# Gather passes of layers 1 and 3 over fixed spans of 128 sorted blocks, summed in a PSUM bank that a register addresses

## The chip, the cores and the metric

The program is one kernel on one core of one Trainium2 chip. It does a whole graph network in one launch. The metric is the device time of an execution in microseconds (us). The kernel before took 3753.84 us, the median of three runs (3752.54 to 3764.85).

The engines are TensorE (PE in the profile, PEld for its weight loads), VectorE (DVE), ScalarE (ACT), GpSimd (POOL) and SyncE (SP). Each runs its own instruction stream and waits for the others through semaphores. A "q" behind a name, as in PEldq, means the engine's sequencer: register loads, address arithmetic, branches.

## The reference, cut to what matters

There are 6250 nodes of 128 features and 100000 edges with source, target, 128 attributes, a type out of three and a weight. Four layers are computed one after the other:

```
v   = segment_sum(edge_attr, src) / count                 # layer 0, then an MLP with batch norm
agg = segment_sum(x[src], dst) / degree                   # layer 1
msg = [x[src], x[dst]] @ Wmsg[edge_type]                  # layer 2
agg = segment_sum(msg, dst) / count
out = segment_sum(dinv[src] * w * dinv[dst] * (x @ W)[src], dst)   # layer 3
```

After each layer come a residual sum and a layer norm. All values are fp32. What matters here is `x[src]` (a gather by source node) and `segment_sum(..., dst)` (a reduction by target node), done once per layer for all edges.

## The kernel before, in words

Nodes lie in 49 groups of 128. An edge belongs to a pair (source group, target group); the edges of a pair are packed into blocks of four. Two DRAM tables hold the blocks: `slots`, sorted by source group, and `gbuf`, sorted by target group. There are at most 26801 blocks. First a placement pass (to 1103 us in the trace) scatters all edges into `slots`, with POOL's indirect DMAs.

A tile is 128 consecutive blocks of a table. Tiles are cut so that each belongs to one group: a group's first tile begins at the group's first block, and its last tile runs over into the next group's blocks. With 49 groups that makes 258 tiles (`TILES`), handled in 43 rounds (`RR`) of 6 (`RING`). Blocks of a tile that aren't the group's own get the address NOWHERE in `to_blk`, and the indirect DMA drops them.

The stages that the change touches are these:

- `reduce(0)`, from about 1110 us: tiles of `slots` are loaded by SP. POOL's `keep_lanes` writes each edge's lane (its source node within the group) into `dst_lane`. DVE and ACT turn lanes into one-hot matrices, PE multiplies and DVE adds to `sums`. Beside that ACT's `keep_pays` copies each tile's payload (8 numbers an edge) into `pays`; one tile in six has its one-hot made by ACT (`scalar_hots`).
- `gather(1)`, from 1467.8 us, and `gather(3)`, from 3086.9 us: for each tile DVE makes a one-hot out of lanes that SP loads again from `lane_rows`. PE waits for the one-hot (`src_hots`) and for a free PSUM bank (`staged`), and does four 128x128 fp32 matmuls into bank r, each one a complete result (`start=True, stop=True`). ACT copies the bank into a ring of six row buffers (for layer 1 with the payload beside it, for layer 3 scaled by the edge's weight). POOL issues one indirect DMA that scatters the 128 rows to their blocks in `gbuf` (`scatter_block`, L804; it prints as `to_blk`). ACT takes a row buffer again when its send has landed (`sent`).
- `gather(2)` is the same by edge type, with bf16 parts. The change leaves it as it is.
- `reduce(1)`, `reduce(2)`, `reduce(3)` read tiles of `gbuf`.

PE has to know which node group a tile belongs to. The number differs with the input, so it comes out of a table in SBUF. At the head of each round of six tiles, `loaded(at_x, ...)` brings six values into PE registers. In the trace that is a TENSOR_LOAD on PE's sequencer (L501). The loop over 43 rounds is a hardware loop (`pe.Fori`), one round an iteration, so the order in the program is: register load, then six times (address arithmetic, waits, four matmuls), then the branch. DVE and SP do register loads of the same kind in the `reduce` stages (`at_sum`, `at_blk`).

## Time and profile before

| | |
|---|---|
| median of 3 timed runs | 3753.84 us |
| span of the profiled execution, first to last instruction | 3754.1 us (the profile gives no other time of it) |
| PE / DVE / POOL / ACT busy | 75% / 67% / 50% / 40% |
| mean granted TensorE clock | 0.961 |
| gather(1): first matmul to start of last send | 1467.8 to 1806.4 us |
| gather(3): first matmul to start of last send | 3086.9 to 3434.0 us |

The profile is one execution. A group of instructions is a row with the line, engine, operation, operands, count, busy time and mean duration, and behind the bar the idle time of the engine before them and what ended it. PE's fp32 matmuls appear as two records each, so one tile of `gather(1)` is 8 records. A row of one source line's instructions gives the minimum, median and maximum duration in ns, and the first and last start.

### The profile page before, as it was taken

What the parts mean: (1) busy time and instruction counts of PE and PEld (TensorE: products, weight loads), DVE (VectorE), ACT (ScalarE), POOL (GpSimd) and SP (SyncE); (2) the same over time, 40 slices, a digit from 0 to 9 for tenths busy, and PEclk for the clock granted to TensorE, in tenths of its full rate; (3) what the DMA queues carried; (4) which work ended last, traced back from release to release, by engine and by line L of the source; (5) the groups of instructions that cost most, each with busy time, mean ns of one, the idle gap of its engine ahead of it and who ended that gap; (6) DMA issues with size and microseconds to landing.
All of it is one profiled execution on the core that took longest, in us unless ns stands there. A gap on an engine that the chain in (4) does not pass through costs nothing.

```text
span 3754.1 us, 95326 instructions
## 1 busy us (share of the span) xinstructions
PE 2826.7 (75%) x23184; PEld 2448.4 (65%) x23185; DVE 2500.2 (67%) x7099; ACT 1518.9 (40%) x4337; POOL 1873.3 (50%) x2268
## 2 busy tenths in 40 slices
PE   8555544444439986778799799999999957777996
PEld 6232322222229965777799479999888957777995
DVE  7666666666647778555577777777666776554667
ACT  0111000000004445555576543222365347887665
POOL 4777777777763342777434344444432007774000
PEclk9999999999999998999899899999999969998998
DMA  6444444444449933888697035555477817786883
GB/s 214 151 149 144 146 149 141 149 143 147 148 130 290 291 128 118 279 275 277 221 290 255 9 127 180 173 183 177 136 226 235 263 38 269 275 275 197 286 281 122
DMA packets 419029, 721.55 MB, mean 192 GB/s; under 512 B 68624, under 2 KB 198169, under 8 KB 417932
## 3 DMA queue, kind: packets, MB, share of 16 engines
q1 hardware_dynamic: 330492, 494.35, 43.0%
q0 software_dynamic: 88464, 226.43, 16.0%
q14 instruction: 52, 0.43, 0.0%
q8 instruction: 21, 0.34, 0.0%
HBM read 481.26 MB, written 285.09 MB: 204 GB/s over the span
## 4 chain that ended last, share of the span: by engine, by line
PE 39%; POOL 23%; issue 14%; DMA 12%; DVE 5%; ACT 3%; SPq 2%; DVEq 1%; POOLq 1%; ACTq 0%
POOL slots L750 19%; PE ps L1379 18%; PE ps L1412 9%; DMA gbuf<-ring_raw,to_blk 8%; PE ps L1414 5%; POOL gbuf L804 4%; DMA ring_raw<-gbuf 3%; PE ps L1254 2%; PE ps L1465 1%; PE ps L1456 1%; SPq L501 1%; SPq L622 1%; DVE stats L1930 1%; PE ps L1521 1%; DVEq L501 1%
## 5 line engine op out<-in xcount | busy, mean ns | idle before, releaser
L804 POOL DMA_INDIRECT gbuf<-ring_raw,to_blk x774 | 754.2, 974 | 728.9 <-DVE ring_raw L1863 261.9
L750 POOL DMA_INDIRECT slots<-ring_raw,idx_edges x782 | 751.4, 961 | 242.3 <-issue 242.3
L1379 PE MATMUL ps<-ring_raw,memory 128*128 128x128 f32 (+2 forms) x6576 | 783.9, 279 | 84.9 <-DVE memory L1831 49.4
L1379 PEld LDWEIGHTS ps<-ring_raw,memory 128*128 128x128 f32 x6576 | 763.3, 192 | 113.1 <-issue 60.3
L1831 DVE TENSOR_TENSOR memory<-dst_lane,lane_ids 128x512 f32<-128x512 f32 x774 | 539.6, 698 | 73.3 <-POOL dst_lane L768 51.1
L1290 PE MATMUL ps<-memory 128*49 128x343 bf16 (+6 forms) x784 | 263.5, 489 | 387.9 <-DVE memory L1727 386.6
L1412 PE MATMUL ps<-memory 128*128 x2752 | 497.7, 273 | 10.2 <-DVE memory L1872 8.0
L1841 DVE TENSOR_TENSOR memory<-memory,ps 128x128 f32 (+2 forms) x1032 | 293.4, 284 | 314.7 <-PE ps L1379 302.6
L936 ACT ACTIVATE memory<-lane_ids,dst_lane 128x128 f32<-128x128 f32 x1032 | 331.0, 395 | 400.3 <-PE ps L1379 263.1
L1414 PE MATMUL ps<-memory 128*128 x2752 | 477.5, 220 | 0.0
L1290 PEld LDWEIGHTS ps<-memory 128*49 128x49 bf16 x784 | 113.9, 159 | 530.7 <-DVE memory L1727 301.9
L1424 PE MATMUL ps<-memory 128*128 x2064 | 270.2, 292 | 88.2 <-ACT ring_raw L977 49.9
L888 ACT COPY ring_raw<-memory 128x49 f32 (+1 forms) x112 | 26.0, 232 | 767.5 <-DMA slots<-ring_raw,idx_edges 767.4
L1424 PE MATMUL ps<-X,memory 128*128 x2064 | 267.0, 290 | 78.3 <-DVE memory L1886 31.0
L1424 PEld LDWEIGHTS ps<-memory 128*128 128x128 f32 x2064 | 255.8, 203 | 102.7 <-issue 101.3
L1424 PEld LDWEIGHTS ps<-X,memory 128*128 128x128 f32 x2064 | 252.8, 202 | 92.7 <-issue 91.8
L977 ACT ACTIVATE ring_raw<-ps,edge_w 128x128 f32<-128x128 f32 x1032 | 277.7, 407 | 68.9 <-issue 48.8
L1412 PEld LDWEIGHTS ps<-memory 128*128 128x128 bf16 x2752 | 269.8, 98 | 47.1 <-issue 15.2
L980 ACT COPY ring_raw<-ps 128x512 f32<-128x512 f32 x258 | 151.3, 586 | 361.9 <-PE ps L1414 361.9
L1863 DVE TENSOR_TENSOR ring_raw<-ring_raw,ps 128x512 f32<-128x512 f32 x258 | 177.5, 688 | 144.7 <-ACT ring_raw L980 144.7
L1414 PEld LDWEIGHTS ps<-memory 128*128 128x128 bf16 x2752 | 269.1, 98 | 2.4
L1886 DVE TENSOR_TENSOR memory<-memory,ps 128x512 f32<-128x512 bf16 x252 | 173.5, 689 | 112.4 <-PE ps L1424 112.4
(283 smaller groups left out, 4801.6 us busy)
## 6 DMA issues: line engine op xcount, KB each, us to landing
ring_raw<-gbuf SPq DMA_DIRECT2D x669, 268.0 KB, 3.7
ring_raw<-in_edge_attr SPq DMA_DIRECT2D x111, 448.0 KB
ring_raw<-slots SPq DMA_DIRECT2D x153, 272.0 KB, 4.0
zr<-lane_rows SPq DMA_DIRECT2D x87, 384.0 KB
zt<-lane_rows SPq DMA_DIRECT2D x87, 384.0 KB
memory<-lane_rows SPq DMA_DIRECT2D x84, 384.0 KB
memory<-slots SPq DMA_DIRECT2D x105, 272.0 KB, 4.0
memory<-gbuf SPq DMA_DIRECT2D x105, 268.0 KB, 3.8
```

The lines of the kernel that those rows point to most:

```text
L750: pool.indirect_dma_start(edges, bass.IndirectOffsetOnAxis(idx_edges[0:n, u, j:j + 1], 0), edge_rows[0:n, u, j, :], None).then_inc(scatter ...
L804: pool.indirect_dma_start(gbuf, bass.IndirectOffsetOnAxis(to_blk[:, t:t + 1], 0), node_rows[:, r, :], None, bounds_check=NBLK - 1, oob_is_ ...
L936: ins = act.activation(hots[:, r, j * P:(j + 1) * P], lane_ids[:, :], ACT.Abs, bias=dst_lane[:, bass.ds(at, 1)], scale=-1.0)
L977: ins = act.activation(rows[:, j, 0:D], parts[:, j, :], ACT.Copy, scale=edge_w[:, bass.ds(at * BLK + j, 1)])
L1290: ins = pe.matmul(counts_of(s)[:, j * GROUPS:].rearrange("p (n g) -> p n g", g=GROUPS), hot2[:, u, 0, :, j], hot2[:, u, 1, :, j][:, None, ...
L1379: ins = pe.matmul(bank(r % 3, width), hots[:, r, j * P:(j + 1) * P], rows[:, j, 0:width], start=j == 0, stop=j == BLK - 1)
L1412: pe.matmul(to.rearrange("p (k d) -> p k d", d=D), hot, msgs[:, 0:2, bass.ds(at[r] + t * D, D)], start=t == 0, stop=False, skip_group_chec ...
L1414: ins = pe.matmul(to[:, D:2 * D], hot, msgs[:, 2, bass.ds(at[r] + t * D, D)], start=False, stop=t == TYPES - 1, skip_group_check=True)
L1424: ins = pe.matmul(bank(r)[:, j * P:(j + 1) * P], hots[:, r, j * P:(j + 1) * P], nodes[:, bass.ds(at[r], D)], start=True, stop=True)
L1831: dve.tensor_tensor(hots[:, r, :].rearrange("p (k d) -> p k d", d=P), lane.broadcast_to([P, BLK, P]), lane_ids[:, None, :].broadcast_to([P ...
L1841: dve.tensor_tensor(to, to, bank(r % 3, width), ALU.add).then_inc(added, 1)
L1863: dve.tensor_tensor(rows, rows, pair_bank(r)[:, :, 0:D], ALU.add).then_inc(staged, 1)
```

## The change

Source tiles are no longer cut at group bounds. A span is 128 blocks of `slots` counted from 0, so there are 210 spans (`SPANS`). A span that holds blocks of two or more groups is worked on in several steps, one for each group; the steps of all spans are 258 again. Every step's matmuls add to the span's PSUM bank (`start=False`). The bank is emptied before, by a one-column matmul with `start=True` (`new_bank`), which each step issues for the bank after its own. Only when the last step of a span is done does ACT copy it and POOL send it: 35 rounds (`SR`) of 6 sends.

The mapping from step to span differs with the input, so four things that were constants or single loads now come from tables through registers: the bank that a step adds to (`at_bank`), the bank to empty (`at_next`), the number of sends that must be done (`free`), and on ACT the number of steps after which a span is whole (`span_steps`). The wait for a free bank now asks for the span five before, not six. Rows of `slots` and the payload grow from 8 to 9 numbers an edge (the ninth is the source lane with the type in it, so that a POOL pass over types goes). `keep_pays` writes by span and saves the target address of each tile first.

```diff
-PAY = 8
-P_ONE, P_TYPE, P_W, P_DST, P_SRC, P_TO = 0, 1, 4, 5, 6, 7
+PAY = 9
+P_ONE, P_TYPE, P_W, P_DST, P_SRC, P_TYPED, P_TO = 0, 1, 4, 5, 6, 7, 8
...
             def keep_pays(h, odd):
                 i = h * 2 + odd
+                at = loaded(at_pay, None, i, ACT_E, (SPANS - 1) * BLK * PAY)
                 for r in range(RING):
                     rows = rows_of(0, r, odd).rearrange("p (k w) -> p k w", k=BLK)
                     wait_rows(act, 0, h, r, odd)
-                    act.copy(pays[:, bass.ds(i * RING + r, 1), :].rearrange("p a (k w) -> p (a k) w", k=BLK),
+                    act.copy(to_of[:, bass.ds(i * RING + r, 1)], rows[:, 0, D + P_TO:D + P_TO + 1])
+                    act.wait_ge(pays_kept, i * RING + (RING + r))
+                    act.copy(pays_raw[:, bass.ds(at[r], BLK * PAY)].rearrange("p (k w) -> p k w", k=BLK),
                              rows[:, :, D:ROW_A]).then_inc(pays_kept, 1)
...
-                def send_tiles(i):
+                def send_round(i):
+                    steps = loaded(span_steps[layer], None, i, ACT_E, RING + GATHERED[3] + TILES)
                     for r in range(RING):
                         at = i * RING + r
-                        act.wait_ge(gathered, i * RING + (RING + base + r + 1))
+                        act.wait_ge(gathered, steps[r])
...
-                for i in range(RR):
+                for i in range(RR if layer == 2 else SR):
                     for r in range(RING):
                         scatter_block(i, r)
...
-                def gather_tiles(i):
+                def new_bank(to):
+                    pe.matmul(ps_flat[:, to], ident_h[:, :], none_h, start=True, stop=True, skip_group_check=True)
+
+                def gather_steps(i):
                     at = loaded(at_x, None, i, PE, (GROUPS - 1) * D)
+                    to = loaded(at_bank, None, i, PE, (RING - 1) * 512)
+                    upon = loaded(at_next, None, i, PE, (RING - 1) * 512)
+                    free = loaded(spans_free[layer], None, i, PE, STAGED[3] + SPANS + 2)
                     for r in range(RING):
+                        pe.wait_ge(staged, free[r])
+                        new_bank(bass.ds(upon[r], 1))
                         pe.wait_ge(src_hots, i * RING + (base + r + 1))
-                        pe.wait_ge(staged, i * RING + (base + r + 1))
                         for j in range(BLK):
-                            ins = pe.matmul(bank(r)[:, j * P:(j + 1) * P], hots[:, r, j * P:(j + 1) * P],
-                                            nodes[:, bass.ds(at[r], D)], start=True, stop=True)
+                            ins = pe.matmul(ps_flat[:, bass.ds(to[r] + j * D, D)], hots[:, r, j * P:(j + 1) * P],
+                                            nodes[:, bass.ds(at[r], D)], start=False, stop=j == BLK - 1,
+                                            skip_group_check=True)
                         ins.then_inc(gathered, 1)
```

The rest of the diff makes the tables on DVE after the placement pass (`span_tables`, some 20 operations on at most 258 columns), splits `send` into `send_spans` and `send_typed`, and moves waits to the new counts (`STAGED`).

On PE, at the head of a round of `gather(1)` and in its first tile, this stands in the program before. ISA is address arithmetic on the sequencer, often with a wait:

```order
L501 TENSOR_LOAD at_x
L1421 REGISTER_ALU
L1424 ISA [waits staged,src_hots]
L1424 MATMUL ps<-X,memory 128x128 x4
L1421 REGISTER_ALU
L1424 ISA [waits staged,src_hots]
L1424 MATMUL ps<-X,memory 128x128 x4
```

And this stands there in the changed program. The four loads are `at_x`, `at_bank`, `at_next` and `free`, which all lie in one tensor's partitions and so print as `at_x`:

```order
L532 TENSOR_LOAD at_x
L532 ISA
L532 TENSOR_LOAD at_x
L532 ISA
L532 TENSOR_LOAD at_x
L532 ISA
L532 TENSOR_LOAD at_x
L1470 ISA [waits staged]
L1470 MATMUL ps<-none,ident_h 128x1
L1480 REGISTER_ALU
L1482 ISA [waits src_hots]
L1482 MATMUL ps<-X,memory 128x128
```

One load at the head of a round became four in a row, and each step got a small matmul and an ISA before each of its four matmuls. The second place is ACT's `keep_pays` in `reduce(0)`. Two tiles of it before:

```order
L948 ISA [waits rows_in0]
L948 COPY memory<-ring_raw 128x32
L948 ISA [waits rows_in1]
L948 COPY memory<-ring_raw 128x32
L948 ISA [waits rows_in2]
```

And the head of a round and two tiles of it now:

```order
L532 TENSOR_LOAD at_msg
L441 ISA
L986 ISA [waits rows_in0]
L986 COPY memory<-ring_raw 128x1
L987 REGISTER_ALU
L988 ISA [waits pays_kept]
L988 COPY memory<-ring_raw 128x36
L986 ISA [waits rows_in1]
L986 COPY memory<-ring_raw 128x1
L987 REGISTER_ALU
L988 ISA [waits pays_kept]
L988 COPY memory<-ring_raw 128x36
```

A register load stands ahead of the round, each tile has two copies, and the second waits until the payload copy before it is done.

## Rows read from the trace of the kernel before

**Rows 1.** The page's head.
```profile
span 3754.1 us, 95326 instructions
```

**Rows 2.** Both gathers, reduce(0), gather(2): busy us by engine, clock, DMA share, GB/s.
```profile
1466.00:1798.00 332.00, 266.98 (x2064) 252.78 (x2064) 177.56 (x259) 173.24 (x511) 243.84 (x251) 0.94 0.78 265
3085.00:3444.00 359.00, 273.62 (x2080) 259.15 (x2081) 197.78 (x323) 281.45 (x1042) 251.77 (x258) 0.92 0.73 249
1108.00:1358.00 250.00, 239.70 (x2028) 233.43 (x2029) 187.77 (x467) 114.62 (x465) 85.11 (x258) 1.00 0.90 287
2177.00:2700.00 523.00, 518.40 (x6164) 475.86 (x6165) 380.86 (x1029) 168.32 (x305) 248.69 (x256) 0.99 0.50 170
```

**Rows 3.** Timeline of both gathers: first matmuls, POOL's sends, the last ones.
```profile
1467.82 6.40 PE L1424 MATMUL ps<-X,memory 128*128 x34 [17.79 <-DVE memory L1886]
...
1475.99 0.97 POOL L804 DMA_INDIRECT gbuf<-ring_raw,to_blk  x1 [0.31 <-issue]
1477.27 0.97 POOL L804 DMA_INDIRECT gbuf<-ring_raw,to_blk  x1 [0.30 <-issue]
...
1806.41 0.97 POOL L804 DMA_INDIRECT gbuf<-ring_raw,to_blk  x1 [0.31 <-issue]
...
3086.90 6.29 PE L1424 MATMUL ps<-memory 128*128 x38 [21.46 <-DVE memory L1886]
...
3433.96 0.97 POOL L804 DMA_INDIRECT gbuf<-ring_raw,to_blk  x1 [0.30 <-issue]
```

**Rows 4.** Timeline of PE in gather(1), 1640 to 1662 us.
```profile
1641.31 1.15 PE L1424 MATMUL ps<-X,memory 128*128 x8 [0.63 <-ACT ring_raw L985]
1643.91 4.73 PE L1424 MATMUL ps<-X,memory 128*128 x40 [1.45 <-DVE memory L1886]
```

**Rows 5.** PE's sequencer by line, 1641.3 to 1643.9 us: min/median/max ns, first and last start.
```profile
L501 PEldq TENSOR_LOAD <-at_x x1: 1753/1753/1753, 1641.8 to 1641.8; - x1
L1421 PEldq ALU_OP  x1: 36/36/36, 1643.6 to 1643.6; - x1
```

**Rows 6.** Register loads of gather(1), gather(3), gather(2), and of DVE in reduce(0) (two single ones first).
```profile
L501 PEldq TENSOR_LOAD <-at_x x43: 819/1526/2653, 1466.4 to 1787.7; - x43
L501 PEldq TENSOR_LOAD <-at_x x43: 822/1730/2961, 3085.7 to 3416.9; - x43
L1430 PEldq TENSOR_LOAD <-at_msg x21: 846/895/1249, 2177.7 to 2665.1; - x21
L501 DVEq TENSOR_LOAD <-at_sum x1: 820/820/820, 1138.8 to 1138.8; - x1
L501 DVEq TENSOR_LOAD <-at_sum x1: 1407/1407/1407, 1144.5 to 1144.5; - x1
L501 DVEq TENSOR_LOAD <-at_sum x43: 811/1069/1427, 1114.3 to 1357.6; - x43
```

**Rows 7.** Waits of gather(2), 2256 to 2632 us: total us, times, longest.
```profile
PEld ps L1412 <- issue: 5.3, 15, 0.7
```

**Rows 8.** Weight loads of gather(2), 2256 to 2632 us.
```profile
L1412 PEld LDWEIGHTS ps<-memory 128*128 128x128 bf16 x1985 | 194.2, 98 | 27.9 <-issue 5.3
```

**Rows 9.** Timeline of ACT in reduce(0), 1200 to 1212 us.
```profile
1201.44 1.28 ACT L936 ACTIVATE memory<-lane_ids,dst_lane 128x128 f32<-128x128 f32 x4 [2.72 <-PE ps L1379]
1202.75 0.72 ACT L940 ACTIVATE memory<-memory,ones 128x512 f32<-128x512 f32 x1
1203.38 0.68 ACT L948 COPY memory<-memory 128x32 f32 x5
1207.49 1.28 ACT L936 ACTIVATE memory<-lane_ids,dst_lane 128x128 f32<-128x128 f32 x4 [3.31 <-PE ps L1379]
```

**Rows 10.** Timeline: POOL's first scatter, then DVE's last table, POOL's last scatter.
```profile
85.14 1.21 POOL L734 DMA_INDIRECT slots<-memory,zero_idx  x1 [50.43 <-issue]
...
1085.16 0.32 DVE L1814 TENSOR_SCALAR at_sum<-back 1x258 int32<-1x258 f32 x1
...
1102.84 0.88 POOL L750 DMA_INDIRECT slots<-ring_raw,idx_edges  x1 [0.30 <-issue]
```

More of the change, by code:

```diff
@@ L58 @@
 HALVES = 2 * RR
+SPANS = -(-MAXB // P)
+SR = SPANS // RING
+assert SR * RING == SPANS and SPANS + GROUPS - 1 == TILES and SPANS * P <= NBLK
+assert all((t * 171) >> 10 == t // RING for t in range(SPANS))
 SCALAR_HOTS = ((5,), (2, 5), (5,), (2, 5))
@@ L497, in tile_cols @@
         def tile_cols(table, k, i, n=RING, span=RING):
-            return table[0:1, k, bass.ds(i * span, n)] if k is not None else table[0:1, bass.ds(i * span, n)]
+            return table[:, k, bass.ds(i * span, n)] if k is not None else table[:, bass.ds(i * span, n)]
         def loaded(table, k, i, engine, top, span=RING):
@@ L1072, in _ @@
                 normalise_step(X, i, x1_ready, Y_CUT)
-            send(1)
+            send_spans(1)
             target_hots(1)
@@ L1151, in _ @@
                 parts(i, i + 1 if i + 1 < STEPS else None)
-            send(2)
+            send_typed()
             def own_in(i, first, count=2):
@@ L1230, in _ @@
                 ins.then_inc(st["g3"]["z"], 1)
-            send(3)
+            send_spans(3)
             act.wait_ge(gathered, RING + GATHERED[3] + TILES)
```

225 lines of the change are left out of this document (145 added, 80 removed).

## The prediction, made before the changed kernel was timed

> **What bounds the kernel now.** I read four views in this order. First the page and the time by stage. The page's span is 3754.1 us [rows 1], 0.3 us from the median of the runs shown, so the sum is made against the span and carried over to the median as it is. In the stretches [rows 2] the two gathers that change are those where neither PE nor the DMA engines are full: PE is busy 267 of 332 us and 274 of 359 us, the DMA share is 0.78 and 0.73. `gather(2)` for comparison has PE busy 518 of 523 us.
>
> Second the timeline of POOL [rows 3]. A send starts every 1.28 us (1475.99, 1477.27): 0.97 us of work and 0.30 us between. 258 of those make 330 us, and from the first matmul to the start of the last send it is 338.6 us in `gather(1)` (1467.8 to 1806.4) and 347.1 us in `gather(3)` (3086.9 to 3434.0). So POOL's issue of sends sets the pace, and fewer sends can only help as far as nobody else is near that pace.
>
> Third, who is near: PE. Its matmuls for one tile take 0.895 us: 40 records in 4.73 us and 8 records in 1.15 us [rows 4], so 32 records in 3.58 us. Six tiles are 5.37 us, and a round of six sends is 7.67 us. That looks like 2.3 us of room in each round. The timeline shows that most of it isn't room: between the 8 records and the 40 there is a hole of 1.45 us, in every round.
>
> Fourth, what the hole is. PE's sequencer [rows 5] starts the register load at 1641.8 and holds it for 1.753 us. The next instruction, the arithmetic of line 1421 that only computes a count to wait for, starts at 1643.6, right behind the load. So the load blocks everything behind it in the stream. The matmuls of the tile before end at 1642.46, and the first of the next starts at 1643.91, 0.4 us after the load. The profile puts the hole down to VectorE, whose one-hots are six tiles ahead; it is the load. PE's round is therefore 5.37 + 1.45 = 6.8 us out of 7.67. PE has 0.85 us of room in a round, and not 2.3.
>
> **The change, part by part. Sends.** 210 times 1.28 us are 268 us a gather, 62 us less than 330. This is what the change could give at most in each. Bytes don't fall: the blocks that were dropped from a tile moved no data, and every block is written once either way. The DMA engines' busy time is 0.78 x 332 = 259 us; at the share of 0.90 that `reduce(0)` reaches [rows 2] it fits in 288 us.
>
> **Register loads on PE.** Each round's one load becomes four in a row, with an address instruction between. What does one cost? In the two gathers the median is 1.53 and 1.73 us, with 0.82 as the least and 2.96 as the most [rows 6]. DVE's loads of six values in `reduce(0)` are two kinds, 0.82 and 1.41 us (the two single rows; all 43 have the median 1.07), which alternate from round to round. The mean of the two kinds is 1.11 us. So six 4-byte values cost 1.11 us on the average in a quieter stage, and some 1.63 us (mean of the two medians) in these gathers, where the load shares the way into SBUF with sends and lane loads. After the change the same bytes are spread over more time, so I take a value nearer to the quiet end, 1.25 us; the ends 1.11 and 1.63 are kept for the range.
>
> The Trainium skill, DMA: Bandwidth & Descriptors, section Latency and other measured facts, gives about 600 ns as the floor of a `tensor_load`; no load here reaches it, the least being 0.81 us. The skill's Runtime: NRT & Kernel Launch, section Instruction fetch mechanics, puts such loads at about 200 ns a register even in bulk, which would make 2.4 us of `gather(2)`'s loads of twelve; the trace disagrees with 0.895 us for them. By that rule four loads would be 4.8 us a round, and the sum below would end at about 4000 us.
>
> **How much of them is covered.** PE's array goes on with queued matmuls while the sequencer loads. In `gather(2)`, where PE is full as it will be here, a load of 0.895 us and 0.4 us of restart leave a hole of 5.3 / 15 = 0.35 us [rows 7]. So 0.94 us is covered. In the row of `gather(1)` it was 0.7 us. I take 0.94.
>
> **Matmuls of a step.** There are still 258 steps of four matmuls. Each gets `new_bank` besides, one bf16 weight load and one column. The nearest rows: 98 ns for a bf16 weight load [rows 8], and 518.4 us / 6164 = 84 ns a matmul in full flow [rows 2]. Value 84 ns, bounds 0 (beside other work) and 182 ns. Six make 0.5 us a round. The granted clock is 0.94 and 0.92 in these gathers, that is some 12% to 16% of the time at 1.2 GHz; six steps then take (5.37 + 0.5) x 1.065 = 6.25 us. The address instructions between the matmuls are about 0.12 us each on the sequencer, by estimate: three instructions stand in the 0.36 us between the load's end and the first matmul [rows 4, 5]. Four are 0.5 us in the 0.98 us of a step's matmuls: covered, as the sequencer is ahead.
>
> **The sum.** A round is 6.25 + 4 x 1.25 + 0.3 (three address instructions) + 0.4 (restart) - 0.94 = 11.0 us, against 7.67 now. 43 rounds are 473 us, and 1.5 us to the start of the last send: 475 us. Against 338.6 and 347.1 us that is 136 and 128 us more, 264 together. POOL needs 4.9 x 1.28 = 6.2 us of the 11 in a round and idles. ACT needs 1.1 us a send in `gather(3)`, where it is busiest, 5.3 us of the 11, and its own new load of about 1.25 us a round of sends fits as well. DVE's one-hots wait for PE. The shallower bank ring (five spans, not six) costs nothing while PE is last: during the 5 us hole the sends drain.
>
> **`reduce(0)`.** ACT works from 1201.44 to 1204.2 and then idles 3.31 us of a round of 6.05 us [rows 9]. The second copy per tile is another 0.21 us, and the wait for the copy before it costs perhaps 0.15 us: 6 x 0.36 = 2.2 us, and the load of 0.8 to 1.4 us, partly beside the 0.72 us activation ahead of it. About 2.9 us against 3.31: hidden, cost 0. If the cover fails, with the load at 1.41 us and twice the waits, it is 0.9 us x 43 = 39 us. Rows of `slots` grow by 4 bytes in 544, 0.7%: nothing while POOL's issue sets the placement's pace and PE that of `reduce(0)`, at most 0.7% of the 1350 us of both, 9 us. The tables: DVE has its last at 1085.5, POOL's last scatter is at 1102.8 [rows 10], and some 20 operations of 0.4 us, 8 us, fit between. POOL's two more payload operations lie ahead of a stretch of 50.4 us in which it idles [rows 10]. Together I put 3 us.
>
> 3754 + 264 + 3 = 4021; I forecast 4020 us. With loads of 1.11 us a round is 10.4 us, and the end is 3970; without `new_bank` and at full clock 0.88 us a round less, 76 us, about 3895. With loads of 1.63 us a round is 12.5 us and the end is 4150. The likeliest case's own range is 3890 to 4150.
>
> **Rivals.** First, on the other side: the four loads overlap, because each only reads SBUF and the address instruction between doesn't need its value. Then they cost one load and three times 0.1 us; with 1.6 us for that load the round is 6.25 + 1.6 + 0.3 + 0.4 - 0.94 = 7.6 us, a gather is 327 + 1.5 us, and the end is 10 + 18 us under now: 3725 us. With a load of 1.1 us it is 3685, and the DMA engines would stop it at about 3650. It decides from the point where the four together cost less than some 2 us. For it speaks that no row has two loads back to back. Against it speak the rows of the sequencer [rows 5]: an instruction that doesn't use the value and yet waited until the load's end.
>
> Second, loads at the page's floor of 0.6 us: the mechanism stays, but as a short stall. From the rows this is the case where loads back to back are cheaper than single ones: 4 x 0.6 = 2.4 us, a round of 8.4 us, 24 and 16 us more a gather, 3795 us. The Trainium skill's DMA page (its section named above) has that floor; no row reaches it.
>
> Third, the gain and the loss meet: loads overlap in part, some 2 us for the four, and the time stays within 0.3% (11 us) of 3754.
>
> Fourth, on top of the forecast: ACT becomes the bound in `reduce(0)`, 39 us more, about 4060 us. It wants waits twice as dear as taken, and moves the time inside the forecast's range.
>
> **How the numbers follow.** Serial loads (with or without the fourth) 0.81, the cheap serial ones 0.04, overlapping ones 0.11, a draw 0.04. Faster by over 0.3% is the overlap, 0.11; within 0.3%, which is about what a measurement of this kernel can tell from no change, 0.04; slower 0.85. The range from 3790 to 4140 leaves out the overlap and the draw, 0.15, and some 0.05 at the ends.
>
> **What would show it.** In the changed profile PE's sequencer should have four register loads in a row at each of 43 rounds, each starting when the one before has ended, and the array should stand still some 4 to 5 us behind them. POOL's sends should come in bursts with idle between, its idle time before sends more than 150 us a gather above now, and PE's matmuls from the first to the last should take some 470 us. The stretches of `gather(2)`, the three later reductions and the placement should be as now. It is wrong if the four loads start together or if a round takes under 8 us; then the first rival holds. If the round is about 11 us but `reduce(0)` has grown by over 10 us, the fourth holds as well.

## The result, and the profile after

The changed kernel takes 4345.9 us (median of 4 runs, 4343.3 to 4356.2), the kernel before beside it 3753.2 us (4 runs): 1.158 times as long, 95% interval 1.157 to 1.160. I had forecast 4020 us, with a range that ended at 4140. The direction was right and the size was wrong by more than half: 593 us more, where 266 were forecast.

The page of the changed kernel: span, granted clock in 40 slices, and PE's two kinds of matmul in the gathers (busy us, mean ns | idle before, and what ended it).

```profile
span 4345.0 us, 98074 instructions
...
PEclk9999999999999777777899999999998677777998
...
L1470 PE MATMUL ps<-none,ident_h 128*128 128x1 bf16 x518 | 96.0, 185 | 544.8 <-issue 507.0
...
L1482 PE MATMUL ps<-X,memory 128*128 x2064 | 364.8, 350 | 3.4
```

Two stretches of sevens in the clock row are new; they are the two gathers. 507 us of PE's idle time stand before the matmul that opens a round, put down to "issue": nothing was waited for but the instruction itself. Both gathers, `reduce(0)` and `gather(2)`, to be held against [rows 2]:

```profile
1481.00:2102.00 621.00, 372.06 (x2319) 353.90 (x2320) 173.94 (x252) 144.37 (x417) 201.23 (x207) 0.73 0.41 141
3392.00:4024.00 632.00, 377.94 (x2318) 359.27 (x2318) 193.53 (x308) 230.24 (x833) 200.49 (x207) 0.73 0.40 138
1114.00:1372.00 258.00, 246.86 (x2059) 239.39 (x2060) 191.83 (x470) 169.67 (x731) 83.34 (x257) 1.00 0.87 278
2478.00:3001.00 523.00, 520.63 (x6186) 477.36 (x6186) 379.46 (x1023) 168.91 (x306) 249.33 (x256) 1.00 0.51 170
```

`gather(2)` is as it was (523 us). The gathers of layers 1 and 3 are 621 and 632 us instead of 332 and 359, and their clock fell from 0.94 and 0.92 to 0.73. From the first matmul to the start of the last send it is 624.0 and 636.6 us (before 338.6 and 347.1 [rows 3]): 285 and 290 us more, 575 of the 593. `reduce(0)` grew by 6.6 us from its first matmul to its last, and the placement by 3.6 us.

The timeline of PE in one round (start, us, x records, [idle before]), against [rows 4]:

```profile
1741.90 0.18 PE L1470 MATMUL ps<-none,ident_h 128*128 128x1 bf16 x1 [4.79 <-issue]
1742.20 2.08 PE L1482 MATMUL ps<-X,memory 128*128 x8
...
1744.14 2.06 PE L1482 MATMUL ps<-X,memory 128*128 x8
...
1746.06 1.83 PE L1482 MATMUL ps<-X,memory 128*128 x8
...
1747.76 1.14 PE L1482 MATMUL ps<-X,memory 128*128 x8
1748.73 0.17 PE L1470 MATMUL ps<-none,ident_h 128*128 128x1 bf16 x1
1748.76 1.14 PE L1482 MATMUL ps<-X,memory 128*128 x8
...
1749.77 1.14 PE L1482 MATMUL ps<-X,memory 128*128 x8
1757.77 0.18 PE L1470 MATMUL ps<-none,ident_h 128*128 128x1 bf16 x1 [6.86 <-issue]
```

The first three steps behind the hole start 1.9 us apart, the last three 1.00 us apart. The windows of those pieces give the reason, in the column of the granted clock (third from the end):

```profile
1741.90:1747.70 5.80, 5.68 (x27) 5.47 (x28) 1.38 (x2) 1.40 (x4) 0.97 (x1) 0.51 0.14 55
1747.70:1750.60 2.90, 2.90 (x28) 2.87 (x28) 2.04 (x3) 0.72 (x3) 1.94 (x2) 1.00 0.56 191
1750.60:1757.70 7.10, 0.30 (x3) 0.11 (x1) 0.72 (x2) 1.27 (x4) 1.94 (x2) 0.76 0.62 218
1757.70:1761.50 3.80, 3.68 (x18) 3.54 (x19) 0.69 (x1) 0.70 (x2) 0.00 (x0) 0.54 0.00 0
```

The clock is at its full level (2.4 GHz) at the end of a round, drops to the half (1.2 GHz) within the hole, and stays there while the next steps already run. The loads of that hole and of the whole of both gathers (min/median/max ns), against [rows 5, 6]:

```profile
L532 PEldq TENSOR_LOAD <-at_x x4: 1646/1947/2297, 1749.3 to 1756.0; - x4
...
L532 PEldq TENSOR_LOAD <-at_x x168: 826/1656/2762, 1487.3 to 2091.4; - x168
...
L532 PEldq TENSOR_LOAD <-at_x x126: 818/1806/2960, 3398.3 to 4012.6; - x126
...
L532 PEldq TENSOR_LOAD <-at_msg x42: 1456/1744/2812, 3406.0 to 4014.0; - x42
```

They run one after the other. Over the 43 rounds of `gather(1)` four loads span 7.28 us on average (1.70 us each), the array rests 5.82 us, and the six steps take 8.75 us: a round of 14.57 us. POOL's sends come in bursts as forecast:

```profile
1738.87 0.97 POOL L840 DMA_INDIRECT gbuf<-ring_raw,group_raw  x1 [0.30 <-issue]
1745.99 0.97 POOL L840 DMA_INDIRECT gbuf<-ring_raw,group_raw  x1 [6.15 <-ACT ring_raw L1021]
```

So my mechanism stood, and two sizes in it didn't: 4.76 us of rest were forecast and 5.82 measured, 6.25 us of steps forecast and 8.75 measured. The theory that I then tested: the loads dominate, directly and through the clock. Its rivals: `new_bank` between the steps, or something else of the change (tables, spans, ACT's waits).

### The profile page after: what moved, and what is told of

It reads as the page before. It is cut to its first block, busy times and chain, and to the rows that moved or that the text cites. A ratio compares the mean times of both kernels' runs of the same rounds, so it can differ in the third digit from the quotient of the medians.

```text
span 4345.0 us, 98074 instructions
## 1 busy us (share of the span) xinstructions
PE 3041.8 (70%) x23700; PEld 2652.2 (61%) x23701; DVE 2510.6 (58%) x7118; ACT 1497.6 (34%) x4308; POOL 1769.2 (41%) x2172
## 4 chain that ended last, share of the span: by engine, by line
PE 49%; issue 19%; POOL 17%; ACT 4%; DMA 3%; DVE 3%; SPq 2%; ACTq 1%; DVEq 1%; POOLq 0%
POOL slots L784 17%; PE ps L1430 16%; PE ps L1482 14%; PE ps L1463 8%; PE ps L1465 4%; DMA ring_raw<-gbuf 3%; ACT ring_raw L1017 2%; PE ps L1304 1%; PE ps L1525 1%; PE ps L1516 1%; SPq L532 1%; DVE stats L2021 1%; SPq L653 1%; PE ps L1581 1%; PE ps L1554 0%
## 5 line engine op out<-in xcount | busy, mean ns | idle before, releaser
L840 POOL DMA_INDIRECT gbuf<-ring_raw,group_raw x420 | 409.0, 974 | 1128.4 <-ACT ring_raw L1017 587.5
L1922 DVE TENSOR_TENSOR memory<-lane_pair,lane_ids 128x512 f32<-128x512 f32 x774 | 541.5, 700 | 77.9 <-POOL lane_pair L807 22.8
L1463 PE MATMUL ps<-memory 128*128 x2752 | 498.1, 273 | 10.1 <-DVE memory L1963 7.7
L1465 PE MATMUL ps<-memory 128*128 x2752 | 477.5, 220 | 0.0
L1470 PE MATMUL ps<-none,ident_h 128*128 128x1 bf16 x518 | 96.0, 185 | 544.8 <-issue 507.0
L973 ACT ACTIVATE memory<-lane_ids,lane_pair 128x128 f32<-128x128 f32 x1032 | 330.9, 395 | 312.7 <-PE ps L1430 244.9
L1017 ACT ACTIVATE ring_raw<-ps,lane_pair 128x128 f32<-128x128 f32 x840 | 232.2, 381 | 411.3 <-PE ps L1482 397.4
L1482 PE MATMUL ps<-memory 128*128 x2064 | 371.1, 354 | 2.6
L1482 PE MATMUL ps<-X,memory 128*128 x2064 | 364.8, 350 | 3.4
L840 POOL DMA_INDIRECT gbuf<-ring_raw,to_blk x258 | 251.6, 975 | 277.5 <-DVE ring_raw L1954 263.3
L1482 PEld LDWEIGHTS ps<-memory 128*128 128x128 f32 x2064 | 350.6, 256 | 13.6 <-issue 0.2
L1463 PEld LDWEIGHTS ps<-memory 128*128 128x128 bf16 x2752 | 269.7, 98 | 47.2 <-issue 15.3
```

Of the source, the lines that this page charges most:

```text
L840: pool.indirect_dma_start(gbuf, bass.IndirectOffsetOnAxis(to[:, t:t + 1], 0), node_rows[:, r, :], None, bounds_check=NBLK - 1, oob_is_err= ...
L973: ins = act.activation(hots[:, r, j * P:(j + 1) * P], lane_ids[:, :], ACT.Abs, bias=dst_lane[:, bass.ds(at, 1)], scale=-1.0)
L1017: ins = act.activation(rows[:, j, 0:D], parts[:, j, :], ACT.Copy, scale=edge_w[:, bass.ds(at * BLK + j, 1)])
L1463: pe.matmul(to.rearrange("p (k d) -> p k d", d=D), hot, msgs[:, 0:2, bass.ds(at[r] + t * D, D)], start=t == 0, stop=False, skip_group_chec ...
L1465: ins = pe.matmul(to[:, D:2 * D], hot, msgs[:, 2, bass.ds(at[r] + t * D, D)], start=False, stop=t == TYPES - 1, skip_group_check=True)
L1482: ins = pe.matmul(ps_flat[:, bass.ds(to[r] + j * D, D)], hots[:, r, j * P:(j + 1) * P], nodes[:, bass.ds(at[r], D)], start=False, stop=j = ...
```

## The experiments

**One part each, in the kernel before.** `head3` puts four loads of `at_x` at the head of a gather round, `head1` two, `spread3` also four but ahead of tiles 0, 1, 3 and 4; `newbank` adds the bank-opening matmul alone.

```diff
-                    at = loaded(at_x, None, i, PE, (GROUPS - 1) * D)
+                    sets = [loaded(at_x, None, i, PE, (GROUPS - 1) * D) for _ in range(4)]
+                    at = [sets[r % 4][r] for r in range(RING)]
```

> The kernel before, with four register loads of the node table in a row at the head of each round of the two gathers in place of one; nothing else (258 sends, no bank matmul). Theory A (serial loads, and a clock that falls in the long hole): a round is as long as in the changed kernel, some 14 us, both gathers grow by about 280 us each, 4300 us in all, and the granted clock in them is near 0.73. Theory B (serial loads, clock no part of it): matmuls at their present pace, round 5.7 + 4 x 1.7 + 0.4 - 0.9 = 12 us, 516 us a gather, about 4100 us. Theory C (the loads overlap or are hidden, and the bank matmul or the address instructions between matmuls are what costs): within 50 us of 3753.

> The kernel before with two register loads in a row at the head of each round of the two gathers. Two loads of 1.6 us leave a hole of about 2.7 us. If the clock stays at some 0.93: round 5.7 + 3.2 + 0.4 - 0.9 = 8.4 us, 361 us a gather, about 3790 us. If a hole of that length already brings the clock down as in the changed kernel: round 5.37 x 1.4 + 2.7 = 10.2 us, 439 us a gather, about 3940 us. Theory C: no change.

> The kernel before with four register loads a round, but one each ahead of tiles 0, 1, 3 and 4 and not all at the head. As many loads as in the run with three more at the head, in four short holes. Each load of 1.7 us and 0.4 us of restart has up to 0.9 us covered by queued matmuls: four holes of 1.2 us, round 5.7 + 4.8 = 10.5 us, 452 us a gather, about 3965 us, with the clock near 0.9. Theory A says it is at least 200 us faster than with all four at the head, since the clock stays up; theory B says that it differs only by the cover, 3 x 0.9 x 86 = 230 us at the most, at an equal clock. If the clock here is near 0.73 as well, then it is the share of idle time and not the length of one hole that counts.

> The kernel before with the one-column matmul ahead of each tile's four and those four adding to the bank (start=False); one register load a round, 258 sends. Theories A and B: six times 84 ns fit in PE's 0.85 us of room in a round, within 15 us of 3753. Theory C: much of the 590 us, at least 200 us.

The rest is the mean over the rounds of `gather(1)`. The first three kernels were timed twice each, `newbank` eight times.

| | median us | ratio (95%) | rest of the array a round | clock in gather(1) |
|---|---|---|---|---|
| head3 | 4169.8 | 1.111 (1.107 to 1.114) | 5.24 us | 0.76 |
| head1 | 3811.8 | 1.015 (1.010 to 1.021) | 2.15 us | 0.89 |
| spread3 | 3848.0 | 1.025 (1.022 to 1.028) | 2.3 us, in pieces | 0.93 |
| newbank | 3754.0 | 1.000 (0.999 to 1.001) | as before | 0.96 |

The same four loads cost 413 us at the head and 91 us spread out. The window 1481 to 1781 us of `head3`, then of `spread3`:

```profile
1481.00:1781.00 300.00, 175.44 (x1104) 171.25 (x1104) 94.71 (x138) 95.67 (x276) 133.88 (x138) 0.76 0.49 164
```

```profile
1481.00:1781.00 300.00, 225.01 (x1609) 205.26 (x1609) 138.07 (x201) 139.46 (x400) 194.22 (x200) 0.93 0.70 239
```

Four loads in a row thus cost 70% as much as the whole change without anything else of it, and the clock falls with the long rest. The 322 us between `head3` and `spread3` aren't the clock alone. Between its own instructions PE's sequencer stands still in `head3` for 4.0 us a round (pauses over 0.15 us counted), while the array works off its steps; in `spread3` it hardly ever does. There it works from end to end, beside the array, and its loads and arithmetic make the round. I had expected four holes of 1.2 us and 3965 us; it was 3848. `newbank` costs nothing while the sends set the pace. Does it still cost nothing behind the loads? `head3bank` has both:

```diff
+                        pe.matmul(bank(r)[:, 0:1], ident_h[:, :], none_h, start=True, stop=True,
+                                  skip_group_check=True)
...
-                                            nodes[:, bass.ds(at[r], D)], start=True, stop=True)
+                                            nodes[:, bass.ds(at[r], D)], start=False, stop=j == BLK - 1,
+                                            skip_group_check=True)
```

> The kernel before with both costs that the change put on TensorE, and nothing else of the change: four register loads in a row at the head of every gather round, and a one-column matmul that opens each tile's bank ahead of its 49 or fewer slice matmuls, which then all add up. Sends, tables and banks stay as before. Theory A (what the change costs is the four loads with the low clock after them, and in the rounds that are now bound by TensorE the bank-opening matmul and the longer steps): about 86 rounds x 0.6 us more than with the four loads alone (4169.75 us), so about 4220 us (4190 to 4260), with about 125 us of the changed kernel's time left for its address instructions, its waits on the register-held send counts and its other stages. Rival B (the bank matmul is free here as it was alone): 4170 us. Rival C (the bank matmul's break between the steps is what brings the clock further down, from 0.77 to 0.73): about 4330 us.

(A tile's matmuls in this kernel are four, and not "49 or fewer".) 4237.7 us, ratio 1.130 (1.128 to 1.132), clock 0.75: 68 us over `head3`, 0.79 us a round. An instruction that is free in one kernel is paid for once its engine is last: six times 84 ns would be 0.5 us at full clock. A round takes 13.44 us here (loads 6.26, all else 7.18) against 14.57 in the changed kernel (7.28 and 7.29). 1.13 us times 86 rounds is 97 of the 108 us still missing, and nearly all of it is load time again: the fourth table has 16-bit values (1.79 us a load by its position, against 1.35), and the others take 1.66 us on average against 1.57.

**The clock by itself.** `warm6` is the changed kernel with six matmuls of 512 columns, read by nobody, ahead of the loads.

```diff
+                    for _ in range(6):
+                        pe.matmul(bank(6), ident[:, :], wcat[:, 0:4, :].rearrange("p g d -> p (g d)"), start=True, stop=True,
+                                  skip_group_check=True)
```

> The changed kernel with six matmuls of 512 columns, whose result nothing reads (they go into the sixth bank), issued ahead of the four register loads of each gather round, so that the array has work while the sequencer loads. Theory A (the low clock in the gathers comes from the array's long rest in each round): with the rest filled by some 5 us of work, the granted clock in the gathers goes from 0.73 to above 0.9, the array part of a round from 8.75 to about 6.3 us, the round from 14.6 to about 12.2 us, and the program takes about 4140 us (4090 to 4200), though it does more work. Rival B (the clock doesn't answer to the rest but to something else, as the loads themselves): the clock stays at 0.73, the junk lies beside the loads, and the time stays at 4350 us or rises by up to the junk's own 5 us a round (4780 us). Rival C (loads wait until the array has emptied): the junk adds its 5 us to each round and the clock rises; the time is about 4350 - 200 + 430 = 4580 us.

```profile
1481.00:1781.00 300.00, 265.84 (x1443) 192.61 (x1442) 90.66 (x133) 72.61 (x210) 100.78 (x104) 0.94 0.44 152
```

4297.0 us, ratio 1.145 (1.143 to 1.148): more work, and 49 us less. The array's rest is 1.48 us, the clock 0.94, and what remains of a round of 13.82 us behind rest and 5.3 us of added work is 7.0 us for the six steps in place of 8.75. That the clock answers to the rest is shown. My number was too hopeful (4140), because the added matmuls took the place of the steps that had been queued beside the loads: the last step ends 0.7 us after the first load has begun, in the changed kernel 1.65 us after, so each round lost about 1 us of cover.

**`reduce(0)`.** `pays` is the kernel before with ACT's extra copy and wait.

```diff
+                    act.copy(local0[:, bass.ds(i * RING + r, 1)], rows[:, 0, D + P_TO:D + P_TO + 1])
+                    act.wait_ge(pays_kept, i * RING + (RING + r))
```

> The kernel before with only the extra copy and the extra wait on ScalarE in the loop that keeps the pay columns, as in the changed kernel, and nothing else. Theory A (the first reduction is bound by ScalarE's loop, so that the copy and the wait make it longer): the first reduction's matmuls take about 258 us in place of 251.7, and the program about 3760 us. Rival B (those 6.6 us come from the ring's changed send order or the tables): the stage stays at 251.7 us and the program at 3754 us.

3755.5 us, ratio 1.001 (1.000 to 1.002), and the stage's matmuls take 251.3 us, as before: theory A fell. The 6.6 us of the changed kernel come from something else in that stage (longer rows, ACT's register load or the ring's order); which, wasn't tried.

**What a load costs.** Fewer loads should be cheaper, I thought. `table1` packs the four tables into one of 16-bit values with one load of 24 values a round, `table2` has two loads of twelve, and `word1` packs three tables as 4-byte values into a load of 18, with the 16-bit load of six behind it.

```diff
-                    at = loaded(at_x, None, i, PE, (GROUPS - 1) * D)
-                    to = loaded(at_bank, None, i, PE, (RING - 1) * 512)
-                    upon = loaded(at_next, None, i, PE, (RING - 1) * 512)
-                    free = loaded(spans_free[layer], None, i, PE, STAGED[3] + SPANS + 2)
+                    got = []
+                    for q in range(LOADS):
+                        got += nc.values_load_multi_w_load_instructions(
+                            at_pe_all[0:1, bass.ds(i * (PER * RING) + q * PER * TILES, PER * RING)], engines=[PE],
```

> The changed kernel with its four PE tables packed in one 16-bit table, so that one register load a round brings all 24 values (layer 3 adds its offset to the send count on the sequencer); everything else of the change stays. Theory A: a load costs by the load and not by the value, so the hole is that of the kernel before, about 1.5 us, the clock is back above 0.9, a round is 6.2 + 1.6 + 0.4 - 0.9 = 7.3 us against 7.67 before, a gather is 316 us; with the 10 us that placement and the first reduction have grown the end is 3753 - 22 - 31 + 10 = 3710 us. If a register costs 0.2 us: a load of 4.8 us, round 10.5 us and more, 3950 us or above. Theory C (bank matmul, address instructions): no less than 4200 us.

> The same with two loads of 12 values each a round. Two loads of 1.6 us: hole 2.9 us, round 6.2 + 3.2 + 0.5 - 0.9 = 9.0 us if the clock stays above 0.9, 388 us a gather, 3753 + 49 + 41 + 10 = 3853 us; with the clock at 0.75 another 1.5 us a round, 3980 us.

> The changed kernel, but its three tables of addresses for TensorE (node column, bank, next bank) are laid side by side as 4-byte values, eighteen a round in one register load; the table of send counts stays 16-bit and is loaded by a second load of six values. Two register loads a round in place of four, and as many values. Theory A (a load of 4-byte values costs little more with eighteen values than with six: twelve take 0.9 us elsewhere in this program): the two loads take about 1.0 to 2.5 and 1.7 us, the array's hole is about 3 us in place of 5.8, the granted clock in the gathers rises from 0.73 to about 0.88, a round takes about 9.5 us in place of 14.6, and the program takes about 3930 us (3850 to 4020). Rival B (the price goes with the values, whatever their width, as it did with the 16-bit tables): the loads take 7 us together as before, and the time stays at about 4350 us. Rival C (sharing a table's place with other engines' tables costs more): slower than 4360 us.

They took 4348.5, 4367.6 and 4242.4 us (ratios 1.157, 1.163 and 1.131, each within 0.003). The one load of `table1`:

```profile
L1484 PEldq TENSOR_LOAD <-at_pe x86: 5671/7502/8320, 1475.1 to 4007.9; - x86
```

and two loads of eighteen 4-byte values of `word1`, in neighbouring rounds:

```profile
L1477 PEldq TENSOR_LOAD <-at_all x1: 5205/5205/5205, 1916.5 to 1916.5; - x1
...
L1477 PEldq TENSOR_LOAD <-at_all x1: 1768/1768/1768, 1930.9 to 1930.9; - x1
```

The expectation of a price per load was wrong: 24 16-bit values take 7.5 us in one load and 7.6 us in the two of `table2` (3.9 and 3.5 us; on average, in `gather(1)`), 0.31 us a value. The changed kernel's four loads, three of 4-byte values and one of 16-bit values, take 7.28 us. The 4-byte values are cheap in every second round and dear in the others. A round's 72 bytes begin at a multiple of 16 only every second time; the six values of 24 bytes behind DVE's turns of 0.82 and 1.41 us [rows 6] do the same. `pad8` tests this: the changed kernel with eight places for six values, so that every round begins at a multiple of 32 bytes.

```diff
-            mark(dve.tensor_scalar(at_x, groups_on[0:1], float(D), -float(D), ALU.mult, ALU.add))
+            mark(dve.tensor_scalar(padded(at_x), by_round(groups_on[0:1]), float(D), -float(D), ALU.mult, ALU.add))
```

> The changed kernel with the same four loads of six values a round, but each table has eight places for a round in place of six, so that a round's values begin at a multiple of 32 bytes (16 in the 16-bit table) and not, in every second round, 8 bytes beside one. Theory A (a load whose values begin off a multiple of 16 bytes costs nearly double: 1.4 against 0.8 us on VectorE and 2.2 against 1.1 us on TensorE, by turns): all rounds are like today's even ones, the four loads take 5.0 us in place of 7.3, the rest of the array 3.6 us in place of 5.8, the clock is about 0.8, the round about 11.8 us, and the program about 4110 us (4050 to 4180). Rival B (the turns come from something else that goes by two rounds, as the buffers or the sends): the loads go on by turns and the time stays at 4345 us.

4256.9 us, ratio 1.133 (1.131 to 1.134). The turns are gone (means of the three 4-byte loads 1.41, 1.08 and 1.23 us, alike in even and odd rounds), the four loads span 6.26 us in place of 7.28, and 89 us are back. It is less than forecast, as the 16-bit load stays at 2.0 us:

```profile
L1481 PEldq TENSOR_LOAD <-at_x x301: 813/1306/2643, 1476.5 to 3922.3; - x151
...
L1481 PEldq TENSOR_LOAD <-at_msg x43: 1467/1993/2785, 3350.8 to 3923.7; - x43
```

**Where the loads stand.** With 16-bit values: `half2` moves the second of `table2`'s two loads ahead of the fourth step; `step6` has six loads of four, each ahead of its step.

```diff
                     for r in range(RING):
+                        if r % AHEAD == 0:
+                            got = nc.values_load_multi_w_load_instructions(
+                                at_pe_all[0:1, bass.ds(i * (4 * RING) + 4 * r, 4 * AHEAD)], engines=[PE],
```

> As the kernel with all loads at the head of the round in two loads of twelve 16-bit values (4367.59 us), but the second of them stands ahead of the fourth step instead of behind the first. Theory A (what is loaded beside issued work costs about 1.5 us less a round, and a rest of some 2 us instead of 5.8 leaves more of the clock): each load takes 3.6 us as before, the array rests twice for 2.2 us, the clock is about 0.85, the round about 12.2 us, the program about 4150 us (4080 to 4230). Rival B (where the loads stand makes no difference, TensorE's sequencer being the bound from end to end): 4370 us. Rival C (each rest brings its own slow steps behind it, now twice a round): the clock stays at 0.73 or falls, and the time is 4300 us or more.

> The changed kernel with TensorE's four tables laid step by step in one table of 16-bit values, and a register load of the four values of one step (node column, bank, next bank, sends) ahead of each step, six loads of four values a round in place of four loads of six values at its head. As many values are loaded; only where they are loaded differs. Theory A (the price goes with the values, some 0.3 us each, and the array's queue of issued matmuls covers about 1 to 1.5 us of a load): each load takes about 1.3 us, a step of the sequencer about 2.0 us, the array rests for some 1 us between steps instead of 5.8 us at once, so that the granted clock stays above 0.9; a round takes about 12.0 us in place of 14.6, the program about 4130 us (4050 to 4200). Rival B (a load has a floor of about 1.7 us here, however few its values): 2.4 us a step, a round 14.5 us, and the time stays at about 4340 us in spite of the clock. Rival C (many short rests bring the clock down as a long one does): clock 0.75 and about 4250 us or more.

`half2`: 4144.5 us, ratio 1.105 (1.103 to 1.106), clock 0.82: 223 us less than `table2` for the place alone, as theory A had it. `step6`: 4225.9 us, ratio 1.126 (1.124 to 1.128), clock 0.83 in `gather(1)` and 0.75 in `gather(3)`. I had expected short rests to keep the clock above 0.9; they don't, and rival C is nearer in its number. But the clock no longer sets the time in these two. PE's sequencer stands still for 3.0 us (`gather(1)`) and 2.2 us (`gather(3)`) a round in `table2`, counted as above, and for at most 0.2 us in `half2` and `step6`: what was gained is time in which it had stood still beside the array's slow steps. A round of `step6` is 13.0 us, six loads of 1.18 us and six times 0.99 us of all else on the sequencer, where I had taken 0.7. Why the clock falls so far with some 3.0 us of rest a round in four pieces, below what `spread3` has with 2.3 us in three, stays open. Both gathers of `step6`:

```profile
1481.00:1950.00 469.00, 345.18 (x1953) 290.08 (x1953) 149.66 (x218) 121.46 (x350) 169.68 (x175) 0.83 0.48 163
3292.00:3750.00 458.00, 331.05 (x1749) 281.28 (x1747) 177.86 (x343) 185.95 (x632) 146.01 (x151) 0.75 0.43 148
```

**Cheap loads.** All four tables as 4-byte values in one (`at_all`), every load at a multiple of 16 bytes. `wordhead` loads 24 values at the head, `wordhalf` twice 12, `wordpair` three times 8, `wordstep` six times 4; `wordtwin` is `wordpair` with two rounds in a turn of the loop.

```diff
+                        if r % AHEAD == 0:
+                            got = nc.values_load_multi_w_load_instructions(
+                                at_all[32:33, bass.ds(i * (4 * RING) + 4 * r, 4 * AHEAD)], engines=[PE],
...
-                        pe.wait_ge(staged, free[r])
+                        pe.wait_ge(staged, (free[r] & 1023) + STAGED[layer])
```

> The changed kernel with TensorE's four tables side by side as 4-byte values, in one load of 24 values at the head of a round that begins at a multiple of 32 bytes in every round. Theory A (4-byte values that begin so are loaded some at a time: eighteen took 2.1 us in every second round and 6.2 us in the others): the load takes about 2.3 us, the array rests about 1.2 us, the clock is above 0.9, the round about 7.8 us, and the program about 3750 us (3700 to 3820). Rival B (each value has its price of some 0.3 us, as the 16-bit ones have): the load takes 7 us and the time is 4340 us.

> The same table of 4-byte values, laid so that two loads of twelve do, each for three steps, ahead of the first and of the fourth step. Theory A (twelve such values take about 1.2 to 1.6 us here, which the array's queue covers): the array rests 0.3 us or less twice a round, the clock stays at 0.95, the round takes 6.3 to 6.8 us where the kernel before takes 7.9, since the 210 sends at 1.28 us a send need only 6.3 us a round; the program takes about 3640 us (3600 to 3720), below the kernel before. Rival B (the sends or ScalarE's copies keep the pace that they had, 7.7 us a round): 3740 us. Rival C (each value has its price): 4140 us, as with 16-bit values in the same places.

> The same table, in six loads of four 4-byte values a round, each ahead of its step. Theory A (a load of four such values costs 0.8 to 1.0 us whatever else, so that a step of the sequencer takes 0.7 + 0.9 = 1.6 us, against 1.0 us of the array): a round of about 9.7 us, 3910 us for the program (3850 to 4000): more loads are worse than two. Rival B (small aligned loads cost in proportion, 0.4 us for four): a step fits in the array's, 3650 us. Rival C (they cost what four 16-bit values did, 1.1 to 1.2 us): 4200 us.

> The table of 4-byte values once more, now in three loads of eight values a round, each ahead of two steps (two loads of twelve took 1.06 us each, six of four 0.47 us each). Theory A (TensorE's sequencer is the bound now, with 0.87 us a step, 1.1 us around a load of twelve and 0.5 us for the loop's branch: measured in the kernel with two loads, at a round of 8.0 us; what is saved is only the rest of the array that the queue doesn't cover): a load takes 0.6 to 0.8 us, the array rests 0.3 us three times, the round takes about 7.5 us, and the program about 3750 us (3730 to 3790). Rival B (loads this small lie wholly beside the issued work): a round of 6.3 to 6.8 us, about 3670 us, and faster than the kernel before. Rival C (each load has a price of its own beside its values, as six of four showed with 3911 us): 3830 us.

> As the kernel with three loads of eight values, and with two rounds in a turn of TensorE's loop, so that it branches 22 times a gather in place of 43. Theory A (the sequencer is the bound): 0.3 us less in every round than with one round a turn, 25 us less for the program, about 3725 us. Rival B (the array or the sends are the bound, or the loop's branch lies beside issued work): the same time within 5 us. Rival C (the longer loop body has to be fetched again and again): slower by 20 us or more.

| | median us | ratio (95%) | values a load, median us | clock in gather(1) |
|---|---|---|---|---|
| wordhead | 3810.6 | 1.014 (1.013 to 1.016) | 24, 2.12 | 0.96 |
| wordhalf | 3802.8 | 1.012 (1.010 to 1.014) | 12, 1.10 | 1.00 |
| wordpair | 3839.2 | 1.022 (1.020 to 1.023) | 8, 0.72 | 1.00 |
| wordstep | 3910.7 | 1.041 (1.039 to 1.043) | 4, 0.34 | 1.00 |
| wordtwin | 3803.8 | 1.013 (1.011 to 1.014) | 8, 0.61 | 1.00 |

The load of 24 in `wordhead`, which carries what took 7.5 us above:

```profile
L1481 PEldq TENSOR_LOAD <-at_all x86: 1614/2116/2929, 1474.9 to 3471.9; - x86
```

Width, place and packing of the values, with all else of the change kept, take off some 535 us (4345.9 to 3810.6); packing by itself gave nothing (`table1`). What is left, 45 us in `wordhalf`, can be read from PE's timeline:

```profile
1702.71 1.14 PE L1494 MATMUL ps<-X,memory 128*128 x8
1704.61 0.17 PE L1475 MATMUL ps<-none,ident_h 128*128 128x1 bf16 x1 [0.77 <-issue]
...
1706.87 1.14 PE L1494 MATMUL ps<-X,memory 128*128 x8
1708.81 0.17 PE L1475 MATMUL ps<-none,ident_h 128*128 128x1 bf16 x1 [0.80 <-issue]
```

Three steps at 1.00 us and a rest of 0.8 us: PE needs 8.0 us a round in `gather(1)` and 8.6 us in `gather(3)`, both at nearly full clock, where the kernel before takes 7.65 and 7.88 us. So the 48 sends that were saved a gather gain nothing, as PE became the bound. It is the sequencer and not the array: between two of its instructions it never pauses for more than 0.22 us in either gather. One instruction shows it too, the arithmetic for the count to wait for, in 300 us of each:

```profile
L1490 PEldq ALU_OP  x225: 32/36/36, 1482.5 to 1780.2; - x113
...
L1490 PEldq ALU_OP  x416: 36/36/36, 3120.7 to 3418.9; - x139
```

`gather(3)` adds its offset and has two of them a step. The second takes 0.10 us of the sequencer with the pause behind it, 0.58 us a round, and its rounds are 0.62 us longer. And `wordtwin`, which only halves the branches, is 35 us faster than `wordpair`, 0.41 us a round. More and smaller loads are dearer again (`wordpair`, `wordstep`), since each adds its own address arithmetic and start to the sequencer. My expectations for `wordhalf`, `wordhead`, `wordpair` and `wordtwin` were 163, 61, 89 and 79 us too low: I took too little for the sequencer. That `wordstep` came out at 3911 us, where 3910 was expected, is luck: its loads took 0.34 us, near rival B's price and not theory A's 0.8 to 1.0, and the sequencer's other work took 1.1 to 1.2 us a step in place of 0.7. No version here beats the kernel before; the nearest, `wordhalf`, is 45 us short of it.

## Why the prediction was wrong, point by point

- What bounds before, and the hole as PE's register load: right, though the hole of 1.45 us isn't in every round. In `gather(1)` the load takes 1.10 us in one round and 2.11 us in the next, on average, and the hole has a mean of 1.03 us. `head1`, `head3` and `spread3` show by adding loads alone that the load makes it.
- "Register loads on PE", four of 1.25 us: this term failed. They took 1.70 us, 7.28 us for four with what lies between. I had rows for this very stage, 1.53 and 1.73 us [rows 6], and took a value nearer a quieter stage because bytes would be spread more thinly. That stage, `reduce(0)`, isn't quieter: its DMA share is 0.90 against 0.78 [rows 2], on another engine. That the load shares a way with the sends no run shows. It didn't become cheaper with less traffic: the DMA share fell from 0.78 to 0.41 and the mean went from 1.60 to 1.70 us. Why aligned loads cost 1.1 us in these gathers and 0.82 us in `reduce(0)` stays open. The two kinds of load that I saw were a hint that I left lying: they were the place of the values (`pad8`). The rest of the array was 1.06 us a round longer than forecast, although 1.46 us of the loads were covered net of the restart, where I had 0.54: 91 us over 86 rounds.
- "Matmuls of a step", at the clock of before: this term failed most. A step at full clock takes 1.00 us (forecast 0.98), but I carried the clock of 0.93 over into rounds with three to four times the rest. 8.75 us against 6.25: 2.5 us a round, 215 us. `warm6` shows that it is the rest that costs the clock. Whether it is the long rest in one piece isn't settled: `spread3` speaks for it, `step6` against it.
- The sum: 3.56 us times 86 rounds are 306 us on top of 4020, with 7 us more in the placement and `reduce(0)`: 4333 us against 4345.9 measured. The rounds of `gather(3)`, 0.27 us longer than the 14.57 us of `gather(1)`, are 12 of the 13 us left.
- Sends in bursts, `gather(2)` and the later reductions as before: right. `reduce(0)` without any cost: 6.6 us off, and not through the ACT copies that I weighed.
- The rivals: loads one after the other was right, overlap wrong. That loads cheaper than these would make a short stall only (3795 us) is what `wordhead` and `wordhalf` then came to, through the width and place of the values.
- The Trainium skill, Runtime: NRT & Kernel Launch, section Instruction fetch mechanics, has about 200 ns a register for such loads; it speaks there of loads from HBM, and those here read SBUF. I set it aside for a row of twelve 4-byte values in 0.895 us. With the 16-bit tables the runs show 0.31 us a value, so that the rule errs there on the low side; with 4-byte values at multiples of 16 bytes it is 0.09 us. And the least load of the kernel before is 0.71 us (SyncE, six values) and not 0.81; four aligned values took 0.33 us in `wordstep`, below the 0.6 us of the second rival.

## What to carry to other kernels

Price an added stall twice: by its length, from rows of the same stage, and by what the array does behind it: here the first two or three steps behind a rest of 5 us and more ran at half clock. Before adding a table for an engine's registers, ask whether the values are four bytes wide and each load begins at a multiple of 16 bytes, and put the loads between pieces of issued work rather than in a row. An instruction measured as free beside another bound has to be priced anew when its own engine becomes the bound.

## What the runs showed of the hardware

- The shortest loads read like groups of four and single values: aligned 4-byte values take 0.33 us for 4, 0.59 for 8, 0.85 for 12 and 1.61 for 24 (0.27 to 0.33 us for each four of them). Six take 0.82 us aligned and 1.41 us 8 bytes off; 16-bit values 0.98 us for four, 2.85 for twelve, 5.67 for 24 (0.24 us each). That four aligned values go at once and all others singly fits all of these and is my reading; only the place (`pad8`) and the width (`table1` against `wordhead`) were varied by themselves, and the two latter differ in place too.
- The rest a round and the granted clock in `gather(1)`: 0.6 us twice, 1.00 (`wordhalf`); 1.3 us, 0.96 (`wordhead`); 2.1 us, 0.89 (`head1`); 5.2 us, 0.76 (`head3`); 4.8 us, 0.75 (`pad8`); 5.8 us, 0.73 (the changed kernel). It is no rule: `step6`, with rests of 0.5 to 1.2 us ahead of most steps, had 0.83 and 0.75, and the kernel before 0.94 with a mean of 1.0 us.
- PE's sequencer needs some 0.87 us for a step with four matmuls at register addresses (`wordhalf`, mean of `gather(1)` without loads and branch), next to 1.00 us of the array. A gather that looks bound by matmuls has little room there for one more load.
